# The loads of the down weight move from SP's queue to ScalarE's, and the opening gets a new order

## The reference

```
x = x + softmax((ln(x) Wq)(ctx Wk)^T / 8, per head) (ctx Wv) Wo + bo        8 heads of 64
x = x + bit(silu(bit(ln(x), w_gate)) * bit(ln(x), w_up), w_down)            512 -> 2048 -> 512
bit(x, w) = act_quant(x) @ weight_quant(w)^T
weight_quant(w): s = 1 / clip(mean|w|, 1e-5); clip(round(w s), -1, 1) / s   (ternary)
act_quant(x): s = 127 / clip(max|x| per row, 1e-5); clip(round(x s), -128, 127) / s
```

## Time and profile before

| | |
|---|---|
| median of 3 runs | 1103.5 us (1101.89 to 1106.36) |
| the profiled execution | 1102.12 us, span 1100.3 us |
| granted TensorE clock, mean | 0.998 |
| busy PE, DVE, ACT, POOL | 1071.3, 965.9, 743.9, 499.6 us |

### The profile page before, as it was taken

One profiled execution on the slowest core, in us unless ns is written; L12 is line 12 of the kernel. 1 busy time (PEld: TensorE's weight loads), 2 busy tenths in 40 slices (PEclk: granted clock), 3 DMA queues, 4 the chain that ended last, 5 costly groups with the idle time before them and its releaser, 6 DMA issues.

```text
span 1100.3 us, 17415 instructions
## 1 busy us (share of the span) xinstructions
PE 1071.3 (97%) x5466; PEld 493.7 (45%) x5528; DVE 965.9 (88%) x2085; ACT 743.9 (68%) x947; POOL 499.6 (45%) x641
## 2 busy tenths in 40 slices
PE   8879999999999999999999999999999999999998
PEld 6444444444444444444444444444444444444443
DVE  5998898998889988888988988888999889998896
ACT  3997767766666677777666677777666666666443
POOL 0256655555454455565444445545543444433110
PEclk9999999999999999999999999999999999999999
DMA  9999655364455644554564454546555564454334
GB/s 351 305 223 167 125 113 111 81 126 93 101 120 114 123 103 90 118 109 89 119 120 112 100 106 109 98 105 120 102 110 106 119 115 98 106 115 92 78 72 100
DMA packets 355963, 133.80 MB, mean 122 GB/s; under 512 B 332448, under 2 KB 332960, under 8 KB 355360
## 3 DMA queue, kind: packets, MB, share of 16 engines
q1 hardware_dynamic: 355872, 132.70, 55.1%
HBM read 34.08 MB, written 16.78 MB: 46 GB/s over the span
## 4 chain that ended last, share of the span: by engine, by line
PE 78%; DVE 10%; ACT 4%; issue 3%; DMA 2%; SPq 1%; POOL 1%; ACTq 0%; DVEq 0%; POOLq 0%
PE ps L1383 34%; PE ps L1402 17%; PE ps L1319 8%; PE ps L1322 8%; PE ps L1320 8%; DMA FF<-FF 2%; DVE FF L1057 1%; DVE hm L1066 1%; PE ps L1312 1%; DVE bns L1043 1%; PE ps L1219 1%; DVE hm L1061 1%; PE ps L1307 1%; SPq L557 1%; PE ps L1250 1%
## 5 line engine op out<-in xcount | busy, mean ns | idle before, releaser
L1383 PE MATMUL ps<-wgT,FF 128*128 128x512 bf16 x1024 | 263.1, 379 | 1.3 <-DMA FF<-FF 0.9
L1383 PE MATMUL ps<-wW,FF 128*128 128x512 bf16 x1024 | 262.8, 379 | 0.4 <-DVE FF L1057 0.3
L1402 PE MATMUL ps<-wW,FF 128*128 128x512 bf16 x962 | 218.9, 379 | 7.0 <-DMA FF<-FF 3.8
L1057 DVE TENSOR_TENSOR FF<-FF,ps 128x512 f32<-128x512 f32 x256 | 173.8, 681 | 48.7 <-ACT FF L834 27.9
L834 ACT ACTIVATE FF<-ps,sgu 128x512 f32<-128x512 f32 x256 | 173.7, 682 | 60.8 <-PE ps L1383 58.7
L843 ACT ACTIVATE FF<-FF,c 128x1024 int16<-128x1024 f32 x128 | 141.4, 1143 | 74.3 <-DVE c L1070 73.7
L692 POOL TENSOR_TENSOR AT<-AT,rd 128x512 f32<-128x512 f32 x64 | 67.7, 1058 | 219.6 <-DVE rd L1102 215.9
L1402 PEld LDWEIGHTS ps<-wW,FF 128*128 128x128 bf16 x1024 | 99.5, 98 | 126.1 <-issue 7.5
L1383 PEld LDWEIGHTS ps<-wW,FF 128*128 128x128 bf16 x1024 | 99.7, 98 | 122.2 <-DVE FF L1057 3.3
L1383 PEld LDWEIGHTS ps<-wgT,FF 128*128 128x128 bf16 x1024 | 97.6, 98 | 123.8 <-issue 5.0
L680 POOL TENSOR_TENSOR xhl<-xn,xhl 128x512 f16<-128x512 f32 x64 | 74.5, 1164 | 82.5 <-ACT xhl L850 82.5
(11 more groups left out here) (145 smaller groups left out, 1743.5 us busy)
## 6 DMA issues: line engine op xcount, KB each, us to landing
xr<-in_x SPq DMA_DIRECT2D x64, 256.0 KB, 2.8
out<-xr SPq DMA_DIRECT2D x64, 256.0 KB, 2.3
FF<-in_L_ffn_w_gate SPq DMA_DIRECT2D x4, 1024.0 KB, 12.3
wW<-in_L_ffn_w_up SPq DMA_DIRECT2D x4, 1024.0 KB, 15.2
FF<-in_L_ffn_w_down SPq DMA_DIRECT2D x4, 1024.0 KB, 6.8
FF<-FF SPq DMA_TRANSPOSE x192, 3.3
MV<-in_L_xattn_Wq SPq DMA_DIRECT2D x1, 1024.0 KB, 8.7
MV<-in_L_xattn_Wo SPq DMA_DIRECT2D x1, 1024.0 KB, 15.5
```

The lines of the kernel that those rows point to most:

```text
L1057: eng.tensor_tensor(hh, hh, U[n % 2][:, :], ALU.mult).then_inc(v_h, 1)
L1383: mm = eng.matmul(bank[n % 2][:, :].rearrange("p (o f) -> p o f", o=4), qxT[:, i % 2, k, :], w[:, 4 * f:4 * f + 4, k, :], start=(k == 0), ...
L1402: mm = eng.matmul(y_bank(i)[:, :], hT[:, i % 2, c, :], wdT[:, c, :], start=(c == 0), stop=(c == 15))
```

## The change

The four `load_down` pieces go from SP's list to ScalarE's, where they stand behind `abs_sum 1 3`, `c_hi 1 0`, `c_hi 1 1` and `hi 0 6`. The opening lists of all five engines are written anew, with the same pieces for the rest (two at the ends, `turn_x 22` and `x_scale 16`, are now listed, too), and the fillers are dealt out anew: 34 of kind `i` and 90 others become 18 and 138. The lists are cut here to their first parts; behind these they go on to step 15.

```diff
@@ -312,7 +312,7 @@
         TERN_T = [[28.7, 30.7, 32.7, 38.8], [43.2, 45.2, 47.2, 49.2], [61.5, 63.5, 65.5, 67.5]]
         FIRST_T = {"stats": 12.0, "rstd": 12.2, "norm": 12.9, "hi": 13.0, "lo": 14.0}

-        KEEP = [('i', 16), ('i', 1), ('i', 1), ('i', 16), ('t', 9), ('t', 15), ('v', 2), ('v', 57), ('u', 7)]
+        KEEP = [('i', 16), ('i', 1), ('i', 1), ('t', 21), ('t', 13), ('t', 15), ('v', 3), ('v', 71), ('u', 15)]
...
         OPENING = {
             "sync": (
-                "load_ctx, load_x 2, load_wk, load_wq, load_gate 0, load_wv, load_gate 3, load_x 0, load_gate 1, "
-                "load_x 1, load_gate 2, load_up 0, load_up 1, load_wo, load_bo, load_up 3, load_x 3, load_up 2, "
-                "turn_x 0, turn_w 0 0, turn_w 0 1, turn_x 1, load_down 0, load_down 1, load_x 4, load_x 5, load_x "
-                "6, turn_x 2, turn_w 0 2, turn_p 0, turn_w 0 3, turn_x 3, load_down 2, load_down 3, turn_w 1 0, "
-                "turn_p 1, turn_x 4, turn_w 1 1, turn_p 2, turn_x 5, turn_w 1 2, turn_q 0, turn_w 1 3, turn_x 6, "
-                "turn_p 3, turn_w 2 0, load_x 9, load_x 7, turn_q 1, turn_w 2 1, load_x 8, turn_p 4, load_x 10, "
-                "turn_w 2 2, turn_q 2, turn_w 2 3, turn_p 5, turn_h 0 1, turn_x 7, turn_h 0 0, turn_p 6, turn_x 8, "
...
+                "load_ctx, load_wk, load_wq, load_x 0, load_gate 0, load_gate 1, load_wv, load_gate 3, load_gate 2, "
+                "load_x 1, load_up 0, load_x 2, load_wo, load_up 2, load_up 1, load_up 3, turn_x 0, turn_w 0 0, "
+                "turn_w 0 1, turn_x 1, load_x 3, load_x 4, load_bo, load_x 6, load_x 5, turn_x 2, turn_w 0 2, "
+                "turn_p 0, turn_w 0 3, turn_x 3, turn_p 1, turn_w 1 0, turn_x 4, turn_w 1 1, turn_p 2, turn_x 5, "
+                "turn_w 1 2, turn_q 0, turn_w 1 3, turn_x 6, turn_p 3, turn_w 2 0, load_x 8, turn_q 1, load_x 7, "
+                "turn_w 2 1, turn_p 4, load_x 9, turn_w 2 2, load_x 10, turn_q 2, turn_w 2 3, turn_x 7, turn_p 5, "
+                "turn_h 0 0, turn_p 6, turn_h 0 1, turn_q 3, turn_h 1 0, turn_x 8, store_y 0, load_x 11, turn_h 1 "
...
-                "constants, rstd 0 0, x_lo 0, rstd 1 0, x_lo 1, add_bo 0, rstd 2 0, p_norm 0, x_lo 2, rstd 3 0, "
-                "p_lo 0, x_lo 3, p_norm 1, rstd 4 0, p_lo 1, add_bo 1, rstd 5 0, x_lo 4, b_lo 4, b_lo 5, p_norm 2, "
-                "rstd 0 1, p_lo 2, x_lo 5, rstd 6 0, p_norm 3, rstd 1 1, add_bo 2, p_lo 3, x_lo 6, b_lo 6, add_bo "
...
+                "constants, rstd 0 0, rstd 1 0, x_lo 0, x_lo 1, rstd 2 0, p_norm 0, rstd 3 0, add_bo 0, x_lo 2, "
+                "rstd 4 0, p_lo 0, rstd 5 0, x_lo 3, p_norm 1, p_lo 1, add_bo 1, rstd 6 0, x_lo 4, b_lo 4, p_norm "
+                "2, add_bo 2, rstd 0 1, p_lo 2, x_lo 5, p_norm 3, b_lo 5, rstd 1 1, x_lo 6, p_lo 3, b_lo 6, p_norm "
+                "4, add_bo 3, rstd 2 1, p_norm 5, add_bo 4, p_lo 4, b_lo 7, rstd 7 0, b_lo 0, rstd 8 0, add_bo 5, "
...
-                "evac 0, evac 2, evac 4, evac 5, evac 6, q_hi 0, q_hi 1, q_hi 2, q_hi 3, abs_sum 0 1, c_hi 0 0, "
-                "c_hi 0 1, abs_sum 0 3, hi 0 0, x_hi 0, hi 0 1, abs_sum 1 0, hi 0 2, evac 11, tern 0 0, evac 12, "
-                "tern 0 1, tern 0 2, evac 13, hi 0 3, abs_sum 1 1, x_hi 1, evac 14, tern 0 3, abs_sum 1 3, expo 0, "
-                "x_hi 2, tern 1 0, o_hi 0, o_hi 1, tern 1 1, p_hi 0, abs_sum 2 0, c_hi 1 0, expo 1, x_hi 3, tern 1 "
-                "2, hi 0 4, tern 1 3, p_hi 1, c_hi 1 1, hi 0 5, abs_sum 2 1, expo 2, b_wide 4, hi 0 6, hi 0 7, x_hi "
-                "4, b_hi 4, abs_sum 2 2, b_wide 5, b_hi 5, expo 3, abs_sum 2 3, p_hi 2, x_hi 5, tern 2 0, quant_x "
-                "0, tern 2 1, p_hi 3, b_wide 6, expo 4, x_hi 6, tern 2 2, b_hi 6, tern 2 3, quant_x 1, b_wide 7, "
-                "expo 5, silu 0 0, silu 0 1, b_hi 7, silu 0 2, quant_x 2, p_hi 4, b_wide 0, silu 0 3, silu 1 0, "
...
+                "evac 0, evac 2, evac 4, evac 5, abs_sum 0 1, evac 6, q_hi 0, q_hi 1, q_hi 2, abs_sum 0 3, c_hi 0 "
+                "0, q_hi 3, c_hi 0 1, x_hi 0, evac 11, evac 12, hi 0 0, hi 0 1, tern 0 0, abs_sum 1 0, hi 0 2, evac "
+                "13, tern 0 1, hi 0 3, abs_sum 1 1, tern 0 2, evac 14, x_hi 1, tern 0 3, abs_sum 1 3, load_down 0, "
+                "expo 0, tern 1 0, tern 1 1, c_hi 1 0, load_down 1, x_hi 2, p_hi 0, abs_sum 2 0, expo 1, o_hi 0, "
+                "tern 1 2, tern 1 3, x_hi 3, o_hi 1, c_hi 1 1, load_down 2, hi 0 4, hi 0 5, b_wide 4, p_hi 1, "
+                "abs_sum 2 1, hi 0 6, load_down 3, hi 0 7, b_hi 4, x_hi 4, expo 2, abs_sum 2 2, b_wide 5, abs_sum 2 "
+                "3, p_hi 2, x_hi 5, expo 3, quant_x 0, b_hi 5, p_hi 3, b_wide 6, x_hi 6, b_hi 6, expo 4, tern 2 0, "
+                "quant_x 1, expo 5, b_wide 7, tern 2 1, tern 2 2, silu 0 0, p_hi 4, b_hi 7, silu 0 1, silu 0 2, "
+                "tern 2 3, silu 0 3, quant_x 2, b_wide 0, silu 1 0, b_hi 0, silu 1 1, p_hi 5, x_hi 7, silu 1 2, "
...
-                "evac 1, max_w 0, evac 3, max_fold 0, max_c 1, abs_sum 0 0, max_take 0, max_c 2, max_c 0, scale_w "
-                "0, stats 0 0, max_c 3, max_fold 1, q_lo 0, max_take 1, scale_c 0, q_lo 1, scales 0, q_lo 2, c_lo 0 "
-                "0, q_lo 3, x_norm 0, abs_sum 0 2, lo 0 0, stats 1 0, lo 0 1, x_norm 1, mean 0, c_lo 0 1, lo 0 2, "
-                "clip 0 0, max_w 1, clip 0 1, max_fold 2, stats 2 0, clip 0 2, stats 3 0, lo 0 3, abs_sum 1 2, "
-                "max_v, s_max 0, x_norm 2, max_take 2, mean 1, clip 0 3, scale_w 1, e_sum 0, max_fold 3, clip 1 0, "
-                "max_take 3, scale_c 1, x_norm 3, o_lo 0, s_max 1, clip 1 1, scales 1, c_lo 1 0, o_lo 1, e_sum 1, "
-                "clip 1 2, stats 4 0, lo 0 4, s_max 2, stats 5 0, lo 0 5, x_norm 4, clip 1 3, c_lo 1 1, lo 0 6, lo "
-                "0 7, s_max 3, e_sum 2, x_norm 5, add_x 0, stats 0 1, e_sum 3, stats 6 0, mean 2, x_scale 0, add_x "
-                "1, stats 1 1, x_norm 6, copy_x 0, s_max 4, clip 2 0, add_x 2, x_scale 1, stats 2 1, clip 2 1, "
-                "s_max 5, x_scale 2, copy_x 1, e_sum 4, clip 2 2, mult 0 0, add_x 3, mult 0 1, e_sum 5, stats 7 0, "
-                "mult 0 2, mult 0 3, clip 2 3, h_part 0, copy_x 2, mult 1 0, h_max 0, mult 1 1, stats 8 0, x_norm "
-                "7, s_max 6, stats 3 1, mult 1 2, add_x 4, mult 1 3, h_part 1, copy_h 0 0, copy_h 0 1, h_max 1, "
...
+                "evac 1, max_w 0, stats 0 0, abs_sum 0 0, max_fold 0, evac 3, max_c 0, max_take 0, scale_w 0, max_c "
+                "2, max_c 1, max_c 3, q_lo 0, q_lo 1, max_fold 1, x_norm 0, max_take 1, scale_c 0, q_lo 2, abs_sum "
+                "0 2, c_lo 0 0, q_lo 3, scales 0, mean 0, c_lo 0 1, lo 0 0, stats 1 0, max_w 1, lo 0 1, lo 0 2, "
+                "clip 0 0, max_fold 2, stats 2 0, lo 0 3, abs_sum 1 2, x_norm 1, clip 0 1, max_v, max_take 2, clip "
+                "0 2, s_max 0, x_norm 2, max_fold 3, clip 0 3, max_take 3, mean 1, scale_c 1, e_sum 0, clip 1 0, "
+                "stats 3 0, stats 4 0, scale_w 1, s_max 1, x_norm 3, c_lo 1 0, stats 5 0, clip 1 1, o_lo 0, e_sum "
+                "1, clip 1 2, scales 1, clip 1 3, o_lo 1, s_max 2, lo 0 4, lo 0 5, stats 6 0, c_lo 1 1, lo 0 6, "
+                "x_norm 4, lo 0 7, s_max 3, e_sum 2, add_x 0, stats 0 1, x_norm 5, mean 2, x_scale 0, add_x 1, "
+                "copy_x 0, e_sum 3, stats 1 1, s_max 4, x_norm 6, x_scale 1, s_max 5, clip 2 0, e_sum 4, add_x 2, "
+                "copy_x 1, stats 2 1, clip 2 1, x_scale 2, e_sum 5, mult 0 0, clip 2 2, add_x 3, mult 0 1, mult 0 "
+                "2, stats 7 0, clip 2 3, mult 0 3, stats 8 0, copy_x 2, x_norm 7, h_part 0, stats 3 1, mult 1 0, "
+                "mult 1 1, h_max 0, mult 1 2, s_max 6, stats 9 0, add_x 4, x_norm 8, mult 1 3, e_sum 6, copy_h 0 0, "
...
-                "setup 6, setup 7, setup 8, setup 9, keep 2, max_turn 1, setup 10, max_spread 1, keep 3, round_X 0 "
-                "0, round_X 0 1, setup 11, total 0, round_X 0 2, round_X 0 3, setup 12, setup 13, max_turn 2, setup "
-                "14, keep 4, scores 0, keep 5, total 1, max_spread 2, max_turn 3, scores 1, keep 6, max_spread 3, "
-                "keep 7, round_X 0 4, scores 2, round_X 0 5, round_X 0 6, keep 8, round_X 0 7, scores 3, attend 0, "
-                "total 2, attend 1, scores 4, attend 2, scores 5, gate_up 0 0, gate_up 0 1, scores 6, round_X 1 0, "
-                "attend 3, gate_up 0 2, gate_up 0 3, gate_up 1 0, gate_up 1 1, gate_up 1 2, attend 4, gate_up 1 3, "
-                "round_X 1 1, gate_up 2 0, gate_up 2 1, round_X 1 2, attend 5, gate_up 2 2, scores 7, round_X 1 3, "
...
+                "setup 6, setup 7, setup 8, keep 2, max_turn 1, setup 9, setup 10, max_spread 1, setup 11, setup "
+                "12, round_X 0 0, total 0, round_X 0 1, setup 13, round_X 0 2, keep 3, round_X 0 3, max_turn 2, "
+                "setup 14, max_spread 2, keep 4, scores 0, keep 5, total 1, max_turn 3, keep 6, max_spread 3, "
```

(18 more changed lines are left out.)

## The result

| | before | after |
|---|---|---|
| median, first comparison | 1102.44 us (1101.46 to 1106.36, 5 runs) | 1112.62 us (1111.37 to 1114.22, 5 runs) |
| ratio, 95% interval | | 1.0085 [1.0066, 1.0104] |
| median, second comparison (e16, in part 4) | 1104.57 us (26 runs) | 1109.76 us (1107.16 to 1115.07, 9 runs) |
| ratio, 95% interval | | 1.0055 [1.0035, 1.0075] |
| profiled execution; span | 1102.12; 1100.3 us | 1112.87; 1111.1 us |

The account below looks back on a forecast made before the run. VectorE, ScalarE and their ordering bound the opening, delaying TensorE's dense stretch. Chain 0, `scores 7` -1.2 and remaining idle -0.6 gave -1.8 us: 1100.3 from the profiled run, 1101.7 from the median; forecast 1101.0, range 1096 to 1107.

Parts of the forecast that it names:

- SP loses four loads: SP's queue in the opening: 4.7 us of queue time saved, but nothing was late by it, so priced at nothing.
- the new orders as a gain of 1.8 us: After `gate_up 0 0`: -1.2 us for `scores 7`, -0.6 us for half of TensorE's remaining idle in 94 to 180 us.
- late-load rival: `load_down 3` lands at 8.2 us or over, `abs_sum 2 3` starts at 82.2 or later: +2.6 us, about 1103; chance 0.20.
- the Trainium skill on rings: Rule against the change: SP and ACT rings alternate packets on the same engines, so the load shares them with `turn_w 1 0`.
- rival on the other side: ScalarE is stopped at `load_down 3`, which waits for `turn_w 0 3`, or by costly issues: 1110 us; chance 0.10.
- the issue price of 2.89 us: ScalarE's load issues cost 2.89 us instead of 0.5: 9.6 us more for four, all on the chain.
- VectorE ready 1 to 3 us sooner: Opening: VectorE is ready for `mean 2` 1 to 3 us sooner than at 82.30 and doesn't bind it.
- Fuller waits may give 0.5 us back: TensorE's fillers, 60 to 94 us, granted clock 0.95: fuller waits may give back 0.5 us, off the chain.
- Differences below 0.5% can't be told from none: Whole kernel time: differences below 0.5%, 5.5 us, can't be told from none.
- the issue price: ScalarE's four moved loads: 0.5 us each to issue, 2.0 us in all.
- `abs_sum 2 3` as what `total 2` waits for: Opening chain: TensorE's largest wait, 3.04 us before `total 2`, comes when ScalarE's last `abs_sum 2 3` ends.
- the signs: Right: `turn_w 2 0` at 94 to 97 us; wrong: `gate_up 0 0` after 96, `abs_sum 2 3` wait over 2, new TensorE waits.

Follow-up runs that it names:

- e16: The changed kernel run again, unchanged, against the kernel before: 1109.76 us, ratio 1.0055.
- e6: The kernel before with only `load_down 2` and `3` issued by ScalarE, behind `hi 0 4`; SP keeps 0 and 1: 1103.76 us, ratio 1.0007.
- e2: The changed kernel with all four loads back on SP, 0 and 1 behind `turn_x 1`, 2 and 3 behind `turn_x 3`: 1107.83 us, ratio 1.0031.
- e3: The changed kernel with `load_bo` back behind `load_wo` in SP's list: 1111.07 us, ratio 1.0066 to the kernel before.
- e4: The changed kernel with the four loads back on SP and `load_bo` back behind `load_wo`: 1107.55 us, ratio 1.0028 to the kernel before.
- e8: e4 with `load_x 3` also back behind `load_up 3`: 1105.40 us, ratio 1.0019 to the kernel before.
- e9: e8 with POOL's old order at the start and ScalarE's `o_hi 0` behind `x_hi 2`: 1105.93 us, ratio 1.0026 to the kernel before.
- e17: The changed kernel with `load_down 0` moved behind `expo 0` in ScalarE's list: 1107.76 us, ratio 1.0038 to the kernel before.
- e1: The kernel before in its old orders, with only the four `load_down` moved to ScalarE: 1111.08 us, ratio 1.0070.
- e11: The kernel before with only `load_down 0` and `1` on ScalarE, placed behind `expo 0`: 1104.48 us, ratio 1.0007.

## Why the prediction was wrong, point by point

- **The step that failed: "SP loses four loads", priced at nothing.** I took the loads out of SP's queue and counted what SP saved. I did not ask beside which transposes they would now be in flight. SP's order had kept both pairs behind `turn_x 1` and `turn_x 3`; in ScalarE's list nothing does. Two loads ahead of a transpose delay it by some 4.5 us (7.8 and 7.9 us to land instead of 3.1 to 3.7), from either queue; behind one, the changed kernel's `turn_x 1` landed after 5.4. And a load from the other queue close behind one can delay it as much (e6's `turn_x 3` 9.0 us, the changed kernel's `turn_w 0 3` 11.8). The term for it should have been a wait of about 3 us each for `scores 1` and `scores 3` (3.14 and 2.92 measured), and 2.6 us more for matmuls at half clock in each, less what is hidden and less what of the clock came from other waits. Even the saving was smaller: the issue of `turn_w 1 0` fell from 7.67 to 5.71 us, not to 3.
- **The second step that failed: the new orders as a gain of 1.8 us.** With the loads back on SP they cost 0.3% (e2). The 1.2 us before `scores 7` were won and 1.00 lost again just ahead of it; of the 2.37 us that TensorE idled in 94 to 180 us I wanted half of the rest back, and they became 3.71.
- **The late-load rival (0.20) had the right collision and the wrong victim.** It priced the landing of `load_down 3` (+2.6 us). The loads did land late, at 6.0 to 10.1 us, but what cost was the transposes beside them: `turn_x 3` 9.5 us, `turn_w 0 3` 11.8. My prediction cited the Trainium skill on rings that take turns on the same engines (DMA: Bandwidth & Descriptors, Queues, rings and completion order), and used it for one side of the sharing only.
- **The rival on the other side (0.10) came near in the number, in part by luck.** "ScalarE is stopped at a load" said 1110 us; measured 1112.62 and 1109.76. One of its conditions came: `turn_w 0 3`, forecast to land by 71, landed at 79.3 (67.49 + 11.8); `load_down 3` left at 79.34, not 74.0, and ScalarE waited 2.12 us for it. Of these 13.4 us against the kernel before (61.54 + 4.4) 6.0 are a later issue, from `x_hi 2`, as said, and from `turn_x 1` and `load_bo`; 7.4 are the collision. But no piece of ScalarE is in the chain between 50 and 90 us; that goes through `turn_x 1`, `load_bo`, POOL and `turn_x 3`. And the issue price of 2.89 us, its other condition, did not come.
- **Not costed at all:** `load_x 3` and `load_bo` behind `turn_x 1`, and POOL's `rstd` pieces ahead of `x_lo`. The first shows in the chain (`x_lo 2` at 61.15 us; in the kernel before 54.65), the second moved `turn_x 0` by 5 us (37.19 us). By the runs they are small: e3, e4, e8 and e9 show 0.1% at most, within their intervals.
- **"VectorE ready 1 to 3 us sooner"** was wrong: what it needs comes from TensorE's `scores`, it waited 4.34 us for `scores 3`, and `mean 2` began at 90.66 us instead of 82.30. "Fuller waits may give 0.5 us back" was wrong too: the clock in 60 to 94 us fell from 0.95 to 0.85.
- **"Differences below 0.5% can't be told from none"** was too wide: the intervals here are 0.12 to 0.25% to each side.
- **Right:** the issue price (0.33 to 0.38 us, I had 0.5), full clock in the dense stretch, and, for the kernel before, `abs_sum 2 3` as what `total 2` waits for. In the changed kernel `total 2` has no wait at all: `scores 3` comes last there. Of the signs, `gate_up 0 0` after 96 us and a new TensorE wait between 100 and 180 us (129.17) came; `turn_w 2 0` left at 104.56 us, not at 94 to 97. ScalarE's wait before `abs_sum 2 3` was 0.76 us, under the 2 that I had named.

## What to carry to other kernels
A queue is also an order: a load that leaves a queue loses its place behind the transfers that it must not get in front of, so list for each moved load the transfers of all queues that are in flight when it leaves or are issued in the next 8 us, and who waits for them. Put the load behind the urgent transpose, by any queue, and not too close: 2.35 us behind it did no harm in e17, 1.0 us behind it did in e6. And take small gains one by one: three local moves measured 0.25% faster, the new orders as a whole 0.3% slower (e2).

## What the hardware showed that I had not expected

- A transpose issued behind 2 MB of loads lands after 7.8 us in the same queue and 7.9 us across queues, 3.1 to 3.7 without them. With the loads close behind it on the other queue it is as slow or slower: 9.0 us in e6; 11.9 us in e1, where one load left 1.6 us ahead of `turn_x 1` and one 0.6 us behind it, and the second took 10.7 us itself; 15.6 us for e1's `turn_w 1 0`, with loads 2 and 3 leaving 0.9 and 1.4 us behind it, and these took 11.9 and 14.2 us. Beside `load_down 2` the issue of `turn_x 3` took 7.38 us.
- A load can leave ahead of work that stands before it in its engine's list. `load_down 0` stands behind `abs_sum 1 3`, yet it left at 44.95 us, before that piece began (46.66, in the rows of its timeline above). `expo 0`, which had to wait itself, held it back: in e11 and e17 the load left 0.06 us after `expo 0` began (49.96 and 48.15 us).
- The length of a wait alone did not tell what the clock would do. It was 0.50 in 51.5 to 58 us of the changed kernel, from within the 3.14 us wait on, and in 63.5 to 66.5 us of the kernel before, behind a wait of 2.47 us; but 1.00 there behind the wait of 3.04 us, and 0.50 in 50 to 53 us of e17, where the waits just before were 1.09 and 0.32 us. Where it was low, `scores 3` took 5.3 us instead of 2.7, so that with its wait of 2.92 us it came to an end 5.5 us later.
